# Order of the loads and splits in a feed-forward stage, and of VectorE's work in a second attention

## What is computed

```
x = x + attention0(layernorm(x), ctx)      # 16 heads, latent keys, rope
x = x + ffn0(layernorm(x))                 # silu(gate) * up, rms norm, projection; ternary weights
x = x + attention1(layernorm(x), ctx)      # below
x = x + moe(layernorm(x))                  # 32 experts, top 8, threshold TAU = 0.05

# ffn0
gate, up = split(x @ ternary(w_gate_up).T);  h = silu(gate) * up
out = rms_norm(h) @ ternary(w_proj).T
# attention1: 16 heads of 32
q = x @ Wq.T;  k, v = split(latent @ Wkv.T)
out = softmax(causal(q k / sqrt(32))) v @ Wout.T
# moe routing
probs = softmax(x @ gate.T);  topv, topi = top_k(probs, 8);  topv = topv / sum(topv) * alpha
active = topv >= TAU, or the largest where none is;  weights = topv * active, divided by their sum
```

## Time and profile before

| | us |
|---|---|
| median of three runs | 1918.53 (1916.3 to 1921.06) |
| profiled execution | 1920.03 |
| its span, first to last instruction | 1918.2 |
| mean granted TensorE clock | 0.919 |
| TensorE busy | 1620.7 |
| VectorE busy | 1215.7 |
| ScalarE busy | 1065.5 |
| GpSimd busy | 641.3 |
| ffn0 | 720.1 to 1051.1 |
| second attention | 1051.1 to about 1351 |

### The profile page before, as it was taken

The page is one execution under the profiler, slowest core; times in us unless marked ns, Lnnn a source line. Parts: engine busy times, 40 slices in busy tenths (PEclk is TensorE's granted clock), DMA queues, the critical chain, the costliest instruction groups (busy, mean ns, idle before and its releaser), DMA issues. The chain is left out here.

```text
span 1918.2 us, 36277 instructions
## 1 busy us (share of the span) xinstructions
PE 1620.7 (84%) x12199; PEld 1033.4 (54%) x12199; DVE 1215.7 (63%) x2713; ACT 1065.5 (56%) x2661; POOL 641.3 (33%) x478
## 2 busy tenths in 40 slices
PE   4868998999999887999997887656379999999993
PEld 3645756656656643555554454444246666666662
DVE  4556797796796784797886667766733333333332
ACT  2436855756746734586675577543645555555552
POOL 3452503503403400000000123121057777777762
PEclk9679999999999998999998799886589999999997
DMA  6850130120120138776686101001435656565536
GB/s 190 254 171 1 31 94 17 34 86 15 34 88 12 38 123 310 241 258 231 208 278 223 54 2 36 27 28 53 117 77 129 135 136 153 135 135 141 130 81 217
DMA packets 143365, 226.61 MB, mean 118 GB/s; under 512 B 37887, under 2 KB 93439, under 8 KB 143062
## 3 DMA queue, kind: packets, MB, share of 16 engines
q1 hardware_dynamic: 113846, 203.01, 33.8%
q0 software_dynamic: 29344, 21.29, 6.8%
HBM read 175.00 MB, written 98.80 MB: 143 GB/s over the span
## 5 line engine op out<-in xcount | busy, mean ns | idle before, releaser
L2689 PE MATMUL g_ps<-ring,xT 128*128 x1572 | 299.6, 326 | 1.0 <-issue 0.9
L996 POOL TENSOR_TENSOR pr<-pr,sm 100x1444 f32<-100x1444 f32 x64 | 166.2, 2597 | 361.7 <-DVE sm L1028 361.7
L2638 POOL DMA_INDIRECT acc<-rows,slot_sources x131 | 207.8, 1586 | 104.8 <-issue 60.6
L2795 DVE SCALAR_TENSOR_TENSOR hf<-sg,g_ps 128x192 f32<-128x192 f32 x131 | 46.4, 354 | 236.1 <-ACT sg L2744 236.1
L2689 PEld LDWEIGHTS g_ps<-ring,xT 128*128 128x128 f16 x1572 | 142.1, 98 | 71.4 <-issue 5.0
L2628 POOL DMA_INDIRECT xg<-xtab,slot_sources x131 | 138.1, 1054 | 87.2 <-issue 84.5
L1023 DVE TENSOR_REDUCE sm<-s_banks 100x2 f32<-100x722 f32 x128 | 115.8, 905 | 75.7 <-PE s_banks L767 75.2
L2711 PE MATMUL d_ps<-ring,hT 128*128 x655 | 162.8, 379 | 0.7 <-ACT hT L2757 0.7
L920 ACT ACTIVATE pr<-s_banks,sm 100x361 f32<-100x361 f32 x256 | 142.3, 568 | 35.1 <-DVE sm L1023 31.0
L767 PE MATMUL s_banks<-kvp,qp 128*100 128x361 f16 x768 | 138.3, 317 | 10.3 <-ACT pr L920 4.7
L2027 POOL MEMSET zero_row<- 128x544 f32 x1 | 0.6, 556 | 388.5 <-POOLq L1280 388.5
(11 more groups left out here) (325 smaller groups left out, 3889.8 us busy)
## 6 DMA issues: line engine op xcount, KB each, us to landing
split_f<-in_gu SPq DMA_DIRECT2D x64, 384.0 KB, 4.1
split_gu<-split_o SPq DMA_DIRECT2D x64, 384.0 KB, 2.9
ring<-split_gu SPq DMA_DIRECT2D x32, 768.0 KB
head<-in_head SPq DMA_DIRECT2D x16, 864.0 KB, 7.1
tern_w<-in_tern SPq DMA_DIRECT2D x48, 256.0 KB, 3.2
split_f<-in_down SPq DMA_DIRECT2D x32, 384.0 KB, 4.0
split_d<-split_o SPq DMA_DIRECT2D x32, 384.0 KB, 3.5
ring<-split_d SPq DMA_DIRECT2D x32, 256.0 KB
```

The lines of the kernel that those rows point to most:

```text
L996: nc.gpsimd.tensor_tensor(pr[:, s % 3], pr[:, s % 3], small[:, s % 3, 2, :].unsqueeze(2).to_broadcast([SEQ, 4, KEYS]), ALU.mult).then_inc( ...
L2638: nc.gpsimd.indirect_dma_start(out=core.acc[i % NACC][:, :], out_offset=bass.IndirectOffsetOnAxis(ap=core.sources[:, i:i + 1], axis=0), in ...
L2689: last = nc.tensor.matmul(g_ps[i % 2][:, 0:2 * INTER], xT[:, i % 2, a * KT + k, :], ring(i, (2 * k + w) * 2 * INTER, 2 * INTER), start=((k ...
```

## The change

In the ffn: the load of the down weights moves from norm_and_load to SP's queue in ffn0, behind the first four split loads; the semaphore clears come behind it; the loads of W1q, W1kv, W1o and lat move behind stores 24 and 28, into the second chunk. The norm, turn, low and first-row steps come one step earlier, and the splits of the down phase are distributed 3, 3, 2, 0 instead of 2, 2, 2, 2 over the tiles, on both engines.

In the second attention: W1q is split in four column slices, and each projection waits for its own; `ln2`'s moments come behind W1kv's low half; the inversion and the output rows move to the end of VectorE's step; the moments and the root of the last norm of chunks 0 to 2 move from the step of the outputs to the next one (`moments_at` gives steps 8, 12, 16), ScalarE's root behind the exponentials; norm rows and logits follow from the new `NORMS_FROM`.

```diff
@@ norm_and_load, SP
-                sp.dma_start(core.wt[:, UNITS - HT:UNITS, :], core.ternary[:, UNITS - HT:UNITS, :]
-                             ).then_inc(core.down_in, 16)
@@
-NORM_AT, TURN_AT, LOW_AT = (6, 8, 10, 12), (8, 10, 12, 14), (9, 11, 13, 15)
-FIRST_AT = (14, 15)
+NORM_AT, TURN_AT, LOW_AT = (5, 7, 9, 11), (7, 9, 11, 13), (8, 10, 12, 14)
+FIRST_AT = (13, 14)
+LATE_SPLITS = (range(HT, HT + 3), range(HT + 3, HT + 6), range(HT + 6, HT + 8), ())
@@ ffn0, SP
-                sp.dma_start(w_f[:, 0:KT, :], t["W1qT"].rearrange("(k p) n -> p k n", p=P)).then_inc(core.w1_in, 16)
...
-                sp.dma_start(core.lat[:, :, :], core.lat_parts).then_inc(core.w1_in, 16)
-                core.clear_first(sp)
                 es.saved.start(sp)
                 for n in range(es.D):
                     es.load(sp, t, n)
+                sp.dma_start(core.wt[:, UNITS - HT:UNITS, :], core.ternary[:, UNITS - HT:UNITS, :]
+                             ).then_inc(core.down_in, 16)
+                core.clear_first(sp)
                 for n in range(NCH * SPLITS):
                     es.store(sp, n)
                     if n + es.D < NCH * SPLITS:
                         es.load(sp, t, n + es.D)
+                    if n == SPLITS:
...
+                    if n == SPLITS + 4:
...
@@ ffn0, ACT
-                        for j in range(HT + 2 * m, HT + 2 * m + 2):
+                        for j in LATE_SPLITS[m]:
                             es.hi(act, c, j)
@@ ffn0, DVE
                         if m:
-                            for j in range(HT + 2 * m - 2, HT + 2 * m):
+                            for j in LATE_SPLITS[m - 1]:
                                 es.lo(dve, c, j)
                         if c + 1 < NCH and m < 2:
                             first_low(c + 1, m + 2)
                         if m < KT - 1:
                             add_rows(c, m)
-                    for j in range(SPLITS - 2, SPLITS):
-                        es.lo(dve, c, j)
@@
+def moments_at(k):
+    return (k + 1) * CB + LAG + 2
+
+NORMS_FROM = [moments_at(k) + (moments_at(k) < BATCH) for k in range(NCH - 1)] + [BATCH + LAG + 1]
+
 def norms_at(s):
-    return [pair_at(s, LAG + 2, BATCH + LAG + 1)] if pair_at(s, LAG + 2, BATCH + LAG + 1) else []
+    return [(k, 2 * (s - first)) for k, first in enumerate(NORMS_FROM) if 0 <= s - first < 2]

 def logits_at(s):
-    return [k for k in range(NCH) if s == ((k + 1) * CB + LAG + 4 if k < NCH - 1 else BATCH + LAG + 3)]
+    return [k for k, first in enumerate(NORMS_FROM) if s == first + 2]
@@ attention1, PE
-                pe.wait_ge(w_lo, 1)
                 for j in range(QK):
-                    if j == KT:
-                        pe.wait_ge(w_lo, 2)
+                    pe.wait_ge(w_lo, min(j, KT) + 1)
                     project_qk(0, j)
@@ attention1, DVE, start
+                for m in range(KT):
+                    n = slice(m * P, (m + 1) * P)
+                    dve.wait_ge(w_hi, m + 1)
+                    nc.vector.scalar_tensor_tensor(wq[:, 1, :, n], w_f[:, 0:KT, n], W1_Q, wq[:, 0, :, n],
+                                                   ALU.mult, ALU.subtract).then_inc(w_lo, 1)
...
+                    if n == 0:
+                        for b in range(CB):
+                            ln2.moments(dve, BATCH - CB + b, b)
+                        ln2.before_root(dve, 0)
@@ attention1, ACT, step
+                    for k in range(NCH - 1):
+                        if s == moments_at(k):
+                            ln.root(act, k)
...
-                        if m:
+                        if m and k == NCH - 1:
                             ln.root(act, k)
@@ attention1, DVE, step
+                    for k in range(NCH - 1):
+                        if s == moments_at(k):
+                            moments(k)
...
-                    if s < BATCH:
-                        invert(s)
                     if s + 1 < BATCH:
                         v_low(s + 1)
...
-                    for k, m in outs_at(s):
-                        add_rows(k, m)
-                        add_rows(k, m + 1)
-                        if m:
...
                     for k, j in norms_at(s):
                         norm_low(k * CB + j)
                         norm_low(k * CB + j + 1)
+                    if s < BATCH:
+                        invert(s)
...
                     for k in logits_at(s - 3):
                         chosen(k)
                         weights(k)
+                    for k, m in outs_at(s):
+                        add_rows(k, m)
+                        add_rows(k, m + 1)
+                        if m and k == NCH - 1:
+                            moments(k)
```

More of the change, by code:

```diff
@@ L1297, in _ @@
                         es.load(sp, t, n + es.D)
+                    if n == SPLITS:
+                        sp.dma_start(w_f[:, 0:KT, :], t["W1qT"].rearrange("(k p) n -> p k n", p=P)
+                                     ).then_inc(core.w1_in, 16)
+                        sp.dma_start(w_f[:, 2 * KT:2 * KT + 2, :], t["W1kvT"].rearrange("p (k n) -> p k n", k=2)
+                                     ).then_inc(core.w1_in, 16)
+                    if n == SPLITS + 4:
+                        sp.dma_start(w_f[:, KT:2 * KT, :], t["W1oT"].rearrange("(k p) n -> p k n", p=P)
+                                     ).then_inc(core.w1_in, 16)
+                        sp.dma_start(core.lat[:, :, :], core.lat_parts).then_inc(core.w1_in, 16)
                 es.drained(sp)
@@ L1909, in _ @@
                     for k, m in outs_at(s):
-                        pe.wait_ge(w_lo, 3)
+                        pe.wait_ge(w_lo, KT + 2)
                         output(k, m)
@@ L1924, in _ @@
                 act.wait_ge(w_in, 64)
-                for out, a, b, scale in ((wq, 0, KT, W1_Q), (wkv, 2 * KT, 2 * KT + 2, W1_KV), (wo, KT, 2 * KT, W1_O)):
+                for m in range(KT):
+                    n = slice(m * P, (m + 1) * P)
+                    nc.scalar.activation(wq[:, 0, :, n], w_f[:, 0:KT, n], ACT.Copy, scale=W1_Q).then_inc(w_hi, 1)
+                for out, a, b, scale in ((wkv, 2 * KT, 2 * KT + 2, W1_KV), (wo, KT, 2 * KT, W1_O)):
                     nc.scalar.activation(out[:, 0], w_f[:, a:b, :], ACT.Copy, scale=scale).then_inc(w_hi, 1)
@@ L2048, in _ @@
             def _(dve):
-                for b in range(CB):
-                    ln2.moments(dve, BATCH - CB + b, b)
-                ln2.before_root(dve, 0)
-                for n, (out, a, b, scale) in enumerate(((wq, 0, KT, W1_Q), (wkv, 2 * KT, 2 * KT + 2, W1_KV),
-                                                        (wo, KT, 2 * KT, W1_O))):
-                    dve.wait_ge(w_hi, n + 1)
+                for m in range(KT):
+                    n = slice(m * P, (m + 1) * P)
+                    dve.wait_ge(w_hi, m + 1)
+                    nc.vector.scalar_tensor_tensor(wq[:, 1, :, n], w_f[:, 0:KT, n], W1_Q, wq[:, 0, :, n],
+                                                   ALU.mult, ALU.subtract).then_inc(w_lo, 1)
+                for n, (out, a, b, scale) in enumerate(((wkv, 2 * KT, 2 * KT + 2, W1_KV), (wo, KT, 2 * KT, W1_O))):
+                    dve.wait_ge(w_hi, KT + n + 1)
                     nc.vector.scalar_tensor_tensor(out[:, 1], w_f[:, a:b, :], scale, out[:, 0], ALU.mult, ALU.subtract
                                                    ).then_inc(w_lo, 1)
+                    if n == 0:
+                        for b in range(CB):
+                            ln2.moments(dve, BATCH - CB + b, b)
+                        ln2.before_root(dve, 0)
                 dve.wait_ge(g_hi, 1)
@@ L2120, in add_rows, with moments @@
                                                    ).then_inc(tb.sem(use), 1)
+                def moments(k):
+                    for n in range(KT):
+                        dve.wait_ge(tb.sem(("rows", k, n)), tb.after(("rows", k, n)))
+                    for bi in range(CB):
+                        ln.moments(dve, k * CB + bi, bi)
+                    ln.before_root(dve, k)
                 def norm_row(b):
@@ L2250, in _ @@
                         norm2_low(BATCH - CB + s - NORM2_FROM)
-                    for k, m in outs_at(s):
-                        add_rows(k, m)
-                        add_rows(k, m + 1)
-                        if m:
-                            for n in range(KT):
-                                dve.wait_ge(tb.sem(("rows", k, n)), tb.after(("rows", k, n)))
-                            for bi in range(CB):
-                                ln.moments(dve, k * CB + bi, bi)
-                            ln.before_root(dve, k)
                     for k, j in norms_at(s):
```

3 lines of the change are left out of this document (removed).

## The result

The changed kernel takes **1943.8 us** (median of four runs, 1941.99 to 1945.95) against 1918.55 before: ratio 1.0124, 95% interval 1.0104 to 1.0144, so 25.2 us slower. The forecast was 12 us slower, 1930.5 us, with a range that ended at 1940. The direction holds; the size is off by a factor of two.

The account below looks back on a forecast made before the run. TensorE, busy 84%, was taken to bound the kernel, with VectorE pacing the ffn's up phase and the attention's steps. The ffn's -6.7 and the attention's +18.65 gave +12.0 us, 1930.5 median, range 1908 to 1940.

Parts of the forecast that it names:

- Start of the ffn: Up to the first down phase: TensorE's stall for the first split load goes, -15.1 us; a layer norm row's stall, -0.8.
- Chunk boundaries: Between ffn chunks: late split loads hold ScalarE ahead of down tile copies, TensorE stalls and its clock falls, +12.75 us.
- Port: Second attention: GpSimd's normalisation holds VectorE's shifts (+7.4 us) and routing operations (+7.8) through the shared port, +15.2.
- Rival (a): Second attention: the port does not hold the shift or routing operations, -15.2 us, so 1915.3; chance 0.17.
- Order of the steps: Second attention, VectorE's queue: moved inversion, moments, routing and output rows, terms +2.0, -0.25, -3.6, -1.35 and +5.7 us.
- The inversion's place: Attention steps: inversion behind v_low, qk_low and norm lows makes VectorE meet v's copy on ScalarE, +2.0 us with small parts.
- Tail: Last outputs of the attention: TensorE waits for a bank freed by output rows behind norm lows and thresholds, +5.9 us.
- (b): Attention's tail and step 14 hidden by a wait that ends later anyhow, -11.6 us, about 1919; chance 0.08.
- (c): Chunk boundaries: splits 20 and 21 land before ScalarE reaches them, no stalls, 1912 or 1909; chance 0.11, 0.07 with (a).
- (d): Chunk boundaries stall without a fallen clock, 1925.5 us; chance 0.47 together with the forecast.
- (e): Second ffn chunk: W1's loads delay a split, up to +9 us, 1939; chance 0.05.
- (f): Start of the ffn: first split load still lands late, behind both weights, +13 us, 1943; chance 0.05.

Follow-up runs that it names:

- ffn_only: The change's norm_and_load and ffn with the second attention of the kernel before; 1917.17 us against 1917.58, ratio 1.0001.
- splits_back: The changed kernel with the down phase's splits again 2, 2, 2, 2 over the tiles and low halves one tile behind; 1925.85 us against 1917.58 before.
- quarter_last: The changed kernel with GpSimd normalising only 4 of 16 heads, inversion left late; start of the attention to the last peaks 221.8 us against 237.5.
- invert_back: The changed kernel with only the inversion put back ahead of v_low in VectorE's step; 1915.51 us against 1917.58 before, ratio 0.9991.
- quarter_back: As quarter_last, with the inversion back ahead of v_low; start of the attention to the last peaks 212.4 us.
- two_back: The changed kernel with the down phase's splits and the inversion's place both undone; 1908.55 us against 1924.06 before, ratio 0.9928.
- three_back: As two_back, with the output rows also back ahead of norm_low, moments still a step later; 1899.98 us, ratio 0.988 to the kernel before.
- first_later: As three_back, but only chunk 0's moments and root come a step later, chunks 1 and 2 as before; 1899.09 us, ratio 0.9904.
- slices_only: The change's ffn with the old splits, and the old attention with only W1q's slices and ln2's moments behind W1kv; 1899.51 us, ratio 0.9913.
- attn_only: The change's second attention with norm_and_load and ffn of the kernel before; 1944.37 us against 1917.58, ratio 1.0157.
- w1_head: As three_back, with the W1 and latent loads again at the head of SP's queue, semaphore clears still late; 1905.76 us in a single run.

## Why the prediction was right or wrong

- **Start of the ffn, -15.1 and -0.8:** right, if 0.7 us too large. 71.5 us became 56.3, -15.2.
- **Chunk boundaries, +12.75, and the low halves, -2.35:** the mechanism is right step by step. In chunk 0 the copy of tile 2 came 23.9 us into the phase (forecast 23.2), split 23 was there at 32.2 (31.3), TensorE's stalls were 1.32 and 3.71 (1.65 and 3.65), ScalarE's waits 6.5 and 6.4 us. **Its size is the first step that failed.** Forecast for the three chunks +10.4; measured +14.5 and +20.5 in the two profiles, +16.0 in ffn_only, +15.0 in the mean of the seven profiles with this ffn. Two things were short. The 5 us for the clock are what three falls like the one at 892.29 lose, one at each boundary; it fell four times in the first profile and five in the second, and the time at half clock rose by 3.4 to 20.5 us over the 6.8 of before, 11.2 in the mean: at 0.6 us each some 2 to 12 us, 6.7 in the mean. That is an estimate from the table at splits_back. Read back along the same table to the 6.8 us of before, the chunks still come out some 8.4 us longer, where the sum has 5.4. By place: product 2 came 42.4, 47.0 and 43.4 us into the down phases, forecast 41.6 each; the second is the one with two falls. A reading was wrong too: at the third boundary product 2 of before comes at 38.92 (977.70), not 37.40, so the three boundaries should have been +11.25. That makes the miss larger.
- **W1 and latent loads, 0 (worst +9):** right; splits_back shows it.
- **End of the ffn, -1.2:** -3.0; a gain I had too small.
- **ffn, -6.7:** -3.7, +1.9 and -3.4 in three profiles. With the splits' distribution undone the ffn takes 321.6 us, 19.1 less than before; the sum without its boundary term is -19.45. So in the ffn that one term carries the miss.
- **Start of the attention, -4.95:** -4.5 and -5.0. Right.
- **Port, +15.2:** right: 15.3 us by the shortened GpSimd operation, up to 4 more if the holds left in quarter_last are counted. The shifts' part was 9.05 us against 7.4: eight were held by 1.0 to 1.09 us and one by 0.5, where I had taken seven by 1.0 and one by 0.4. The Trainium skill ("SBUF — State Buffer", section "Who interferes with whom") describes an exclusive lock that tensor_scalar can take too, and the rows agree. Rival (a) falls: that all 16 shifts had one length before was because only two met GpSimd, for its last 0.12 us (at 1181.25 and 1191.85), less than their own length.
- **Order of the steps:** the sum of +2.0, -0.25, -3.6, -1.35 and +5.7 is +2.5. With the port's 15.2 and the start, the forecast to the last peaks was +12.75; measured +14.9 and +16.2. The net of the order, some +4.2, is near **by luck**: two errors offset each other. **The inversion's place, +2.0, is the second step that failed**: the quarter runs show 9.3 us (up to 4 of them holds). I had laid the 2.0 into steps 0 to 6, where they show none; it costs 3.6 in steps 8 to 11 and 6.1 in steps 12 to 14, where the queue also holds norm rows and routing. Everything else in the order, forecast +0.5, gained 5.3: that is invert_back against before, less the start. By steps: 0 to 6 forecast +7.15, measured +6.3 and +8.2; step 7 -3.6 and -3.6; steps 12 to 14 +13.5 and +11.2. Steps 8 to 11, forecast +0.65, took +5.5: +3.0 port, +3.6 the inversion's place, -1.1 the rest. VectorE's waits for ScalarE's copies of v and q there are 6.6 and 2.8 us in quarter_last; in quarter_back it waits 0.7 for q and, at the inversion, 4.1 for the exponentials. The held shift also keeps the probabilities from TensorE; its stall in step 9 grows from 1.65 us (before, at 1182.44) to 4.14,

```profile
1184.16 1.52 PE L1786 MATMUL t_bank<-w_kv,lat 128*100 128x512 f16 x3 [4.14 <-DVE pT L2122]
```

and the projections behind it then run at half clock. Peaks 8 to 12, in the changed kernel (first) and before, in us, busy times and, third from the end, the clock:

```profile
1168.23:1233.91 65.68, 49.71 (x665) 31.41 (x666) 44.29 (x82) 41.23 (x148) 15.89 (x8) 0.84 0.11 32
```

```profile
1167.77:1227.94 60.17, 44.51 (x664) 29.33 (x664) 42.58 (x99) 42.27 (x154) 15.91 (x8) 0.95 0.10 32
```

  The same matmuls take 5.2 us more. But that is not what costs the 5 us: in quarter_back they take 49.79 us at a clock of 0.86, and the steps take 59.1 us, less than before. Nor does the clock set the time from the first to the last peaks as a whole: invert_back and quarter_back come to 195.8 and 195.6 us there with 49.5 and 63.2 us at half clock, two_back to 194.9 with 39.8 (its steps 0 to 6, at 0.98 in place of 0.87, took 73.8 us in place of 76.5).
- **Tail, +5.9:** +8.3, **the third step that failed**. The wait for the bank is there (5.12 us, 5.2 in the working), and the outputs' 24 matmuls behind it take 2.4 us longer where the sum leaves 0.7 for the clock. But putting the output rows back returned only 3.7 us (two_back to three_back). What the sum had at nothing is the later norms and logits: 3.1 us for chunks 1 and 2 (first_later) and 2.0 for chunk 0 (slices_only).
- **Attention, +18.65:** +23.2, +24.5 and, in attn_only, +25.2.

The forecast's two halves miss in the same direction, by 5.0 us in the ffn and 5.7 in the attention, but not for one reason. In the ffn the stalls were placed to 1 us in the first chunk, and what went wrong is what the three boundaries cost together: by the estimate above some 3 us more for the waits, and for the clock, which falls more than once a boundary and not equally often in each execution, 1.7 us more in the mean and up to 7 in one execution. In the attention the port was sized right, and the misses are two places in VectorE's queue: the inversion behind the low halves, and the norms and logits behind the last peaks. With ffn -1.7 (mean of the three) and attention +24.3, the sum is +22.6; the other 2.6 us to the measured 25.2 are within what the first attention and the experts vary from one execution to the next, and stay unassigned. Rivals (b), (c), (d), (e) and (f) did not come about.

**A faster kernel** comes out of it: the change without the splits' and the inversion's moves and with the output rows in their place (three_back, 0.988, or first_later, 0.9904) is 18 to 24 us faster than before, and some 44 us faster than the change. slices_only (0.9913), with none of the later moments, can't be told from them.

## What to carry to other kernels

Before an instruction that starts another engine is moved, look at what its own engine does next while that one works: a 0.8 us inversion put directly ahead of the peaks had GpSimd at work when nine of sixteen shifts and part of the routing came, and cost 24 us here and 31 in the kernel before, some 15 of the 24 by the shared port and the rest by its place in the queue. A stall on TensorE's path is to be priced with the clock that falls behind it only where TensorE sets the pace, as at the chunk boundaries (about 0.6 us for each us at half clock); in the attention's steps, which VectorE's queue sets, a lower clock cost little. Work that waits for a DMA must not stand in a queue ahead of the copy that frees the matmuls' banks.

## What the runs showed that was not expected

- The price of one misplaced instruction: `invert` alone, moved in the kernel before, cost 31.6 us of 1924 (invert_last), more than the change as a whole.
- The hold ends with GpSimd's operation, whatever the held instruction's own size: an operation of 1600 values in 100 partitions (2.86 us) and one of 800 (1.52 us) differ by whether they reach the shift, which starts 1.63 us behind GpSimd. 16 values a partition took 1.26 us in place of 0.17.
- The unchanged first attention ended anywhere between 707.5 and 716.4 us, and one build of ffn_only ran between 1905 and 1921 us. Differences of under 5 us between two single profiles of this kernel can't be read from their totals, and in the ffn not from the stage either: its length moved over 11 us between seven profiles of the same code.
- With 3.4 MB more ahead of it, a load of 0.38 MB was used 12.9 us after its issue in place of 6.3 (w1_head and three_back).
